# Values projected from the normalized rows, deviation and mean put back by GpSimd and the gates, and the turned rows kept in two buffers

## The reference

```python
x_norm = layernorm(x) * gamma + beta
q, k   = l2norm(x_norm @ w_q), l2norm(x_norm @ w_k)      # per head
v      = x @ w_v                                         # from x itself, not from x_norm
res    = 0.5 + 0.5 * tanh((q @ k.T - 0.27) * 15)
gate_q = 0.25 + 0.75 * sigmoid(q . g_q);  gate_k likewise
fused  = (res * gate_q * gate_k) @ v
x      = layernorm(x + fused @ w_o + b_o)
x      = layernorm(x + ffn(x))                           # a gated layer on FP4-rounded operands
```

## Time and profile before

| what | value |
|---|---|
| three runs, median (lowest to highest) | 4381.3 us (4379.77 to 4382.84) |
| the profiled execution, its own time | 4378.88 us |
| its span, first to last instruction | 4377.1 us |
| PE, DVE, ACT, POOL busy, share of the span | 94%, 36%, 92%, 4% |
| the first stage | to about 306 us of the span |

### The profile page before, as it was taken

The page is one execution under the profiler, slowest core; times in us unless marked ns, Lnnn a source line. Parts: engine busy times, 40 slices in busy tenths (PEclk is TensorE's granted clock), DMA queues, the critical chain, the costliest instruction groups (busy, mean ns, idle before and its releaser), DMA issues.

```text
span 4377.1 us, 69385 instructions
## 1 busy us (share of the span) xinstructions
PE 4111.8 (94%) x28776; PEld 1285.9 (29%) x28776; DVE 1561.6 (36%) x4540; ACT 4017.1 (92%) x3271; POOL 159.5 (4%) x120
## 2 busy tenths in 40 slices
PE   7988899999999999999999999999999999999997
PEld 5651222222222222222222222222222222222223
DVE  6754023333333332333233333333333333333236
ACT  4669999999999999999999999999999999999993
POOL 2330000000000000000000000000000000000001
PEclk9999999999999999999999999999999999999998
DMA  4454444344434443444334433443345334433450
GB/s 114 124 129 78 70 76 65 61 68 78 65 63 67 78 68 60 66 78 71 60 63 78 77 55 62 78 78 56 61 78 78 56 61 78 78 59 59 77 83 13
DMA packets 179871, 313.70 MB, mean 72 GB/s; under 512 B 65264, under 2 KB 141808, under 8 KB 154608
## 3 DMA queue, kind: packets, MB, share of 16 engines
q1 hardware_dynamic: 179568, 309.41, 42.1%
HBM read 266.82 MB, written 42.47 MB: 71 GB/s over the span
## 4 chain that ended last, share of the span: by engine, by line
PE 69%; ACT 23%; DVE 4%; issue 3%; DMA 1%; SPq 1%; POOL 0%; POOLq 0%; DVEq 0%; ACTq 0%
PE ps L1268 35%; ACT room L706 22%; PE ps L1258 20%; PE ps L1295 8%; PE ps L1318 4%; DMA m_f<-fused_t 1%; DVE room L858 1%; PE ps L1213 0%; DVE st L812 0%; DVE xnT L848 0%; PE ps L1224 0%; PE ps L1308 0%; DVE sm L773 0%; DVE sm L774 0%; DVE sm L775 0%
## 5 line engine op out<-in xcount | busy, mean ns | idle before, releaser
L706 ACT ACTIVATE room<-ps 128x1024 f32<-128x1024 f32 (+1 forms) x2816 | 3787.1, 1417 | 178.4 <-PE ps L1258 162.2
L1268 PE MATMUL ps<-room,vt 128*32 128x512 f32 x16384 | 2051.2, 601 | 0.0
L1258 PE MATMUL ps<-qs,room 64*128 64x512 f16 x8198 | 1325.9, 383 | 203.7 <-ACT room L706 182.6
L1258 PEld LDWEIGHTS ps<-qs,room 64*128 64x128 f16 x8198 | 310.4, 93 | 1749.5 <-ACT room L706 1123.1
L1268 PEld LDWEIGHTS ps<-room,vt 128*32 128x32 f32 x16384 | 388.1, 108 | 945.3 <-issue 945.3
L1295 PE MATMUL ps<-wguT,m_xqT 128*128 128x352 f32 x960 | 348.2, 485 | 0.0
L967 DVE TENSOR_TENSOR vz<-ps,vz 128x352 f32<-128x352 f32 x120 | 63.0, 525 | 757.7 <-ACT vz L716 757.7
L972 DVE TENSOR_TENSOR vz<-ps,vz 128x352 f32<-128x352 f32 x120 | 63.0, 525 | 595.9 <-PE ps L1295 595.9
L1318 PE MATMUL ps<-wdnT,wqk 128*128 128x256 f32 x720 | 198.9, 404 | 0.6 <-DVE wqk L937 0.6
L1295 PEld LDWEIGHTS ps<-wguT,m_xqT 128*128 128x128 f32 x960 | 162.6, 189 | 105.2 <-issue 54.3
L600 POOL TENSOR_TENSOR m_x<-m_x,bo 128x256 f32<-128x256 f32 x60 | 43.9, 731 | 3876.7 <-DMA m_x<-in_L_attn_x_dram 3876.7
(11 more groups left out here) (172 smaller groups left out, 2198.0 us busy)
## 6 DMA issues: line engine op xcount, KB each, us to landing
room<-k_parts SPq DMA_DIRECT2D x520, 256.0 KB, 9.4
vt<-v_gated SPq DMA_DIRECT2D x65, 1024.0 KB, 17.9
qs<-q_parts SPq DMA_DIRECT2D x520, 32.0 KB, 10.1
gqb<-q_gates SPq DMA_DIRECT2D x256, 64.0 KB, 2.2
room<-in_L_attn_x_dram SPq DMA_DIRECT2D x16, 512.0 KB, 4.1
v_gated<-vz SPq DMA_DIRECT2D x64, 128.0 KB, 2.2
fused_t<-fs SPq DMA_DIRECT2D x256, 32.0 KB, 1.7
q_parts<-room SPq DMA_DIRECT2D x30, 256.0 KB, 2.4
```

What stands on the lines that cost most here:

```text
L706: act.activation(res[:, c, o:o + m, :], ps[:, o:o + m, :], ACT.Sigmoid, scale=2 * SHARP / QK_UP ** 2, bias=-2 * SHARP * THRESH).then_inc(b ...
L1258: ins = pe.matmul(ps[:, BANK[n % 2] + i, :], ks[o:o + HROWS, par, h // 2, kt * P:(kt + 1) * P], qs[o:o + HROWS, par, h // 2, :], start=Tru ...
L1268: ins = pe.matmul(ps[32 * h:32 * h + 32, SUM_BANK, :], vt[:, par, n * HD:n * HD + 32], r, start=kt == 0, stop=kt == KT - 1, skip_group_che ...
```

## The change

The values are no longer projected from x but from the normalized rows before gamma and beta (`xh`), which TensorE has turned for q and k anyway. Since x = xh * deviation + mean, the value of a row is deviation * (xh @ w_v) + mean * (sum of w_v's rows), and this is taken as deviation * (xh @ w_v + (mean / deviation) * sum). VectorE makes the two factors per row (`deviations`), GpSimd multiplies the sum of the weights by the second one and adds it to the evicted values, and the first one goes into the gates of the values. The sum of the weights' rows is a product with ones on TensorE ahead of the steps.

The eight transposes of x per block fall away. The transposes of `xh` for block k + 1 (`turn`) are now made in step k, ahead of the last tile, and both tiles made of them, `xnT` on VectorE and `xT` on ScalarE, have two buffers (the second one in memory of weights that come later). VectorE and ScalarE take the two banks in opposite order. The load of x waits for `xh` in place of the transposes.

```diff
@@ -91,7 +91,7 @@
 FFN_LOADS = 5
-A_CHAIN = 14
+A_CHAIN = 15
 RING = 8
@@ -197,12 +197,19 @@
 
+        wguT_flat = wguT[:, :, :].rearrange("p c n -> p (c n)")
+        xnT2 = [xnT[:, :, :], carve(wguT_flat, 0, [DC, BLK])]
+        xT2 = [xT[:, :, :], carve(wguT_flat, DC * BLK, [DC, BLK])]
         last_pt = [carve((xT, xnT)[r // 2][:, :, :].rearrange("p c n -> p (c n)"), r % 2 * BLK, [2, BLK], FP16)
...
         sm = sb("sm", [P, 6, NS + TB])
+        dev = sb("dev", [P, 2, 2, TB])
 
@@ -219,6 +226,12 @@
         a_vg = sem("a_vg")
+        a_dev = sem("a_dev")
+        a_vm = sem("a_vm")
+        a_vmul = sem("a_vmul")
+        s_ones = sem("s_ones")
+        s_ws = sem("s_ws")
+        s_wsum = sem("s_wsum")
         a_pt = sem("a_pt")
@@ -252,6 +265,10 @@
         m_xn = sb("m_xn", [P, D])
+        ones = m_x[:, 0:P]
+        wsum = m_xn[:, :]
+        vm = carve(wdnT[:, :, :].rearrange("p j n -> p (j n)"), 0, [TB, D])
         m_e = sb("m_e", [P, D])
@@ -429,7 +446,7 @@
                 if has(k + 2, 0, NBLK):
-                    wait(sp, a_tr, 2 * (k + 1))
+                    wait(sp, a_xh, k + 1)
                     sp.dma_start(xin[:, par].rearrange("p (t d) -> p t d", t=TB), x_blk[k + 2]).then_inc(a_x[par], 16)
@@ -577,6 +594,7 @@
             pool.tensor_copy(idb[:, :], idf[:, :]).then_inc(s_id, 1)
+            pool.memset(ones, 1.0).then_inc(s_ones, 1)
 
@@ -584,6 +602,15 @@
                     return
+                if isinstance(n, int) and n == 0:
+                    pool.wait_ge(s_wsum, 1)
+                wait(pool, a_ev, TB * (n + 1))
+                wait(pool, a_dev, n + 1)
+                pool.tensor_tensor(vm, wsum.unsqueeze(1).to_broadcast([P, TB, D]), bcast(dev[:, par, 1], D), ALU.mult)                    .then_inc(a_vmul, 1)
+                pool.wait_ge(a_vmul, n + 1)
+                ins = pool.tensor_tensor(vz[:, par, :, 0:D], vz[:, par, :, 0:D], vm, ALU.add)
+                ins.then_inc(a_vm, 1)
+                pool.wait_ge(a_vm, n + 1)
                 v = vz[:, par, :, 0:D].rearrange("p t (h d) -> p t h d", d=HD)
@@ -669,10 +696,6 @@
 
-                if has(k, 0, NBLK):
-                    wait(act, a_tr, 2 * (k + 1))
-                    wait(act, a_qkv, TB * k)
-                    act.copy(xT[:, :, :], ps[:, 2:4, :]).then_inc(a_xT, 1)
                 parts(0)
@@ -686,8 +709,19 @@
                 parts(3)
+                if has(k + 1, 0, NBLK):
+                    turned(k + 1, 1 - par)
                 tile(3)
 
+            def turned(k, par):
+                wait(act, a_tr, k + 1)
+                wait(act, a_qkv, TB * (k - 1))
+                act.copy(xT2[par][:, 1, :], ps[:, 1, :]).then_inc(a_xT, 1)
+                wait(act, a_xnT, 2 * k + 1)
+                act.copy(xT2[par][:, 0, :], ps[:, 0, :]).then_inc(a_xT, 1)
+            turned(0, 0)
             a_steps(act.Fori, a_step)
@@ -839,15 +873,23 @@
 
+            def deviations(k, par):
+                dve.tensor_tensor(dev[:, par, 0], sm[:, 0, NS:], sm[:, 1, NS:], ALU.mult)
+                dve.tensor_tensor(dev[:, par, 1], mv[:, :, 0], sm[:, 1, NS:], ALU.mult).then_inc(a_dev, 1)
+            def turned(k, par):
+                wait(dve, a_tr, k + 1)
+                wait(dve, a_qkv, TB * (k - 1))
+                for c in range(DC):
+                    if c:
+                        wait(dve, a_xT, 2 * k + 1)
+                    dve.tensor_scalar(xnT2[par][:, c, :], ps[:, c, :], gam[:, c:c + 1], bet[:, c:c + 1],
+                                      ALU.mult, ALU.add).then_inc(a_xnT, 1)
             def a_step(k, par):
                 n, m, other = k - 1, k - 2, 1 - par
-                if has(k, 0, NBLK):
-                    wait(dve, a_tr, 2 * k + 1)
-                    wait(dve, a_qkv, TB * k)
-                    for c in range(DC):
-                        ins = dve.tensor_scalar(xnT[:, c, :], ps[:, c, :], gam[:, c:c + 1], bet[:, c:c + 1],
-                                                ALU.mult, ALU.add)
-                    ins.then_inc(a_xnT, 1)
                 if has(n, 0, NBLK) or has(k + 1, 0, NBLK):
@@ -871,11 +913,24 @@
                     wait(dve, a_gt, n)
-                    dve.tensor_scalar(gate.rearrange("p t n -> p (t n)"), sm[:, 5, 0:NS], 0.75, 0.25,
-                                      ALU.mult, ALU.add).then_inc(a_gate, 1)
+                    after(dve.tensor_scalar(gate.rearrange("p t n -> p (t n)"), sm[:, 5, 0:NS], 0.75, 0.25,
+                                            ALU.mult, ALU.add))
+                    gv = gate[:, :, H:2 * H]
+                    dve.tensor_tensor(gv, gv, bcast(dev[:, other, 0], H), ALU.mult).then_inc(a_gate, 1)
+                if has(k + 1, 0, NBLK):
+                    wait(dve, a_vm, n + 1)
+                    if has(n, 0, NBLK):
+                        wait(dve, a_gate, n + 1)
+                    deviations(k + 1, other)
+                    turned(k + 1, other)
 
...
             norm_x(0, 0)
+            deviations(0, 0)
+            turned(0, 0)
+            dve.wait_ge(s_ws, 1)
+            dve.tensor_copy(wsum, ps[:, GT_BANK, 0:D]).then_inc(s_wsum, 1)
             for k in range(4):
@@ -1177,8 +1232,11 @@
                         wait(pe, (a_hi, a_lo)[r // 2], m + 1)
-                    if r == 3 and K:
-                        wait(pe, a_xT, k + 1)
+                    if r == 2:
+                        wait(pe, a_evD, m)
+                    else:
+                        wait(pe, a_evA, 3 * m + r - r // 3 - 2)
                     for i in range(2):
@@ -1190,8 +1248,9 @@
                         wait(pe, a_gate, m + 1)
-                        if K:
-                            wait(pe, a_xT, k + 1)
+                        wait(pe, a_gT, m)
+                        if isinstance(k, int) and k == 2:
+                            pe.wait_ge(s_wsum, 1)
                         for t in range(TB):
@@ -1202,40 +1261,20 @@
                         for c in range(DC):
-                            pe.matmul(ps[:, 4 + t % 2, :], xnT[:, c, tok], wqk[:, c, :], start=c == 0, stop=c == DC - 1)
+                            pe.matmul(ps[:, 4 + t % 2, :], xnT2[par][:, c, tok], wqk[:, c, :], start=c == 0, stop=c == DC - 1)
                         wait(pe, a_ev, TB * k + t)
                         for c in range(DC):
-                            pe.matmul(ps[:, 6, D:D + 2 * H], xnT[:, c, tok], wdot[:, c, :],
+                            pe.matmul(ps[:, 6, D:D + 2 * H], xnT2[par][:, c, tok], wdot[:, c, :],
                                       start=c == 0, stop=c == DC - 1)
                         if t == 0:
-                            wait(pe, a_xT, k + 1)
+                            wait(pe, a_xT, 2 * k + 2)
                         for c in range(DC):
-                            ins = pe.matmul(ps[:, 6, 0:D], xT[:, c, tok], wv[:, c, :], start=c == 0, stop=c == DC - 1)
+                            ins = pe.matmul(ps[:, 6, 0:D], xT2[par][:, c, tok], wv[:, c, :], start=c == 0, stop=c == DC - 1)
                         ins.then_inc(a_qkv, 1)
 
-                if M:
-                    wait(pe, a_evA, 3 * m - 1)
-                    wait(pe, a_evD, m)
-                if K:
-                    wait(pe, a_xh, k + 1)
-                    wait(pe, a_xnT, k)
-                    for c in range(DC):
-                        for t in range(TB):
-                            ins = pe.transpose(ps[:, c, t * P:(t + 1) * P], xh[:, t, c * P:(c + 1) * P], idf[:, :])
-                    ins.then_inc(a_tr, 1)
-                if M:
-                    wait(pe, a_evA, 3 * m)
-                    wait(pe, a_gT, m)
-                if K:
-                    wait(pe, a_xT, k)
-                    for c in range(DC):
-                        for t in range(TB):
-                            o = t * D + c * P
-                            ins = pe.transpose(ps[:, 2 + c, t * P:(t + 1) * P], xin[:, par, o:o + P], idf[:, :])
-                    ins.then_inc(a_tr, 1)
                 parts(0)
                 if K:
-                    wait(pe, a_xnT, k + 1)
+                    wait(pe, a_xnT, 2 * k + 2)
                 tile(0)
@@ -1243,10 +1282,30 @@
                 parts(3)
+                if has(k + 1, 0, NBLK):
+                    turn(k + 1)
                 tile(3)
 
+            def turn(k):
+                wait(pe, a_xh, k + 1)
+                wait(pe, a_xnT, 2 * k)
+                wait(pe, a_xT, 2 * k)
+                if has(k - 3, 0, NBLK):
+                    wait(pe, a_evA, 3 * (k - 3) + 2)
+                    wait(pe, a_evD, k - 2)
+                for c in range(DC):
+                    for t in range(TB):
+                        ins = pe.transpose(ps[:, c, t * P:(t + 1) * P], xh[:, t, c * P:(c + 1) * P], idf[:, :])
+                ins.then_inc(a_tr, 1)
             pe.wait_ge(s_id, 1)
+            turn(0)
+            pe.wait_ge(s_ones, 1)
             pe.wait_ge(s_wdot, DC)
+            for c in range(DC):
```

(2 more changed lines are left out.)

## The result

The changed kernel takes 4412.7 us (median, 4409.9 to 4416.3), the kernel before 4380.6 us in the same rounds: a ratio of 1.0073, with a 95% interval of 1.0056 to 1.0090. It is slower, by 32 us. The forecast was 4393.4 us, 12 us slower, so the direction was right and the size was not; the result lies above the range of 4364 to 4409.

A forecast was written before the change was run, and what follows sets the result against it. A ring through VectorE, ScalarE and TensorE bounds the first stage, 17.39 us a step; thirteen steps of 18.06 plus first and last steps add 12.1 us, giving 4391.0 profiled, plus 2.4 for the median: 4393.4 us, range 4364 to 4409.

The forecast's parts named there:

- The ring without a hold: First stage, each step's loop through VectorE, TensorE and ScalarE from reduction to next reduction: 16.26 us, against 17.39 before.
- the way to the turn: Term of the 16.26 ring: VectorE from reduction to the end of copy L867, 10.56 us, then 0.13 to TensorE.
- The hold and its ring: First stage: GpSimd's two new instructions make VectorE's inverse roots wait; the engines take turns, 18.06 us a step.
- the addition: GpSimd's second new instruction, adding two full operands of 1024 columns: taken as 2.04 us, bounds 1.93 and 2.92.
- The lost race: Rival, much slower: GpSimd starts before VectorE's deviations and delays the turned rows; 21.1 us a step, 4433 us, chance 0.13.
- such a stretched deviation: Sign that would prove the forecast wrong: a lengthened deviation product on VectorE ahead of the turned rows, 21 us a step.
- the cover that the forecast named: 5.6 us of turn, tile 3 and evictions, beside which VectorE's turned rows and statistics were to cost nothing.
- faster: Rival: GpSimd's instructions don't hold VectorE's nine products; 16.26 us a step, 4365 us; faster rivals together 0.16.
- half held: Rival, no change: VectorE is held about 1 us a step, total within 8.8 us of now; chance 0.10.
- TensorE doesn't bound by its amount of work either: Answers the rival that TensorE bounds: removed transposes save 0.88 us in 15 steps, 4368 us; inside faster's 0.16.
- the ring's term for TensorE: Part of the 16.26 ring, from turn through tile 3: transposes 0.88 us, then 2.14 + 1.11 as undisturbed.
- forecast 318.0: Predicted start of the attention, after the first stage: 318.0 us, against 305.95 before, 12.1 us more.

The follow-up runs named there:

- the filled run: The whole change plus products of weights nobody reads on TensorE ahead of the turn (two, three in step 1): 4400.6 us, ratio 1.0043 against the kernel before.

## Why the forecast was right in direction and wrong in size

**The ring without a hold, 16.26:** right to the hundredth, by the run without GpSimd's two instructions. The exactness is luck in part: its terms are off by up to 0.06 (tile 3 took 3.19 instead of 3.25, the way to the turn 10.71 instead of 10.69, the turn 0.91 instead of 0.88) and cancel.

**The hold and its ring, 18.06:** right in mechanism, and 0.34 short. Clear of the clock (the filled run) the ring is 18.40, and the addition was the term mis-sized: 2.35 to 2.37 us, where 2.04 was taken from a subtraction with the bounds 1.93 and 2.92. In the changed kernel itself a step behind a long one is shorter, 18.01, because GpSimd is then done with its gate work before the reduction (idle 0.90 ahead of L609).

**The lost race:** it didn't come; VectorE's first deviation starts at 207.08, GpSimd's gate multiply at 207.12. But GpSimd got in before the second, which was held for 1.91 us. The forecast had such a stretched deviation only as a sign of the lost race, at 21 us a step; it cost nothing here, because the deviations and the turned rows stand in the cover that the forecast named, of which 0.44 us were left in a short step.

**The rivals faster and half held:** out, by the same rows. TensorE doesn't bound by its amount of work either: the filled run gives it 1.94 us more a step and is faster.

**The step that failed** is the ring's term for TensorE: "eight transposes 0.88; tile 3 as an undisturbed tile has it, 2.14 + 1.11". That TensorE would be idle ahead of the turn stood in the forecast, and was priced at nothing. From the turn's start to the end of tile 3's last product (L1272) it took 5.79 us in the step shown (206.72 to 212.51) instead of 4.13: the granted clock, still 1.00 through the wait and the turn (204.30 to 207.60), fell behind them. This happened in eight of thirteen steps at some 1.7 us, and in step 1, where the turn waited 3.42 us, the clock fell during the wait, and the product behind it took 3.62: that step is 20.03 us instead of 16.86, and 17.41 with TensorE kept busy.

The bill at the start of the attention: forecast 318.0, measured 337.95. Of these 20 us, 13.2 are the difference to the filled run (337.95 against 324.74). Of them 0.76 stand already at the first reduction (40.20 against 39.44), ahead of any wait that was filled, so that some 12.4 are the clock: 2.6 in step 1, 10.3 in steps 2 to 14, and 0.5 given back in step 15. In the filled run 4.6 are the longer addition (56.85 to 296.20 against 13 times 18.06), and 2.2 the first two steps and the end. So without the clock the forecast would have been some 7 us short, and the direction was not luck.

## What to carry to other kernels

When a change makes TensorE wait, look for its longest unbroken wait and what runs right behind it, and price that at half clock as well; a wait that was never in the old trace has no price there, and that is a reason for a wider bound, not for zero. A short wait is no guarantee: one of 1.60 us cost the clock once. Work that holds another engine is best moved to one that holds nobody (here ScalarE's four activations) or beside a reduction, and an engine kept busy with work that nobody reads can be cheaper than an idle one.

## What the runs showed of the hardware that was not expected

- Waits of TensorE in one piece, in steps 2 to 14: behind 0.69, 1.22 and 1.81 us the clock never fell; behind 2.24, 2.45 and 2.54 us it fell in some steps and not in others, the same product taking 1.88 or up to 3.56 us; behind 2.84 and 2.85 us in the changed kernel it fell all five times. Length alone doesn't settle it, though: in step 1 a wait of 3.25 us was followed by 1.88 (the run in which GpSimd writes only), one of 3.33 by 3.58 (the run with fills beside the product), one of 3.42 by 3.62 (the changed kernel), and one of 1.60 by 2.77 (the run without GpSimd's two instructions). 2.6 us in two pieces left the clock up. In the eight long steps of the changed kernel the clock was still 1.00 at the end of the wait and fell 0.1 to 1.2 us later, while TensorE was busy again. The Trainium skill (TensorE: Matmul & The Clock Gate, "The HAM clock gate") says that what watches the engine's activity is free-running and doesn't reset when a kernel starts; equal waits with unequal ends agree with that, and no run here shows it directly.
- Fills, which read nothing, held VectorE's scalar instructions of 0.2 us for up to 2.09 us, three fills on end.
- GpSimd's addition of two full operands takes 2.34 to 2.37 us for 1024 columns where its multiply with a broadcast operand takes 1.89 to 1.93.
